# Attention over image rows on one core: P x of two groups between their score matmuls, and its copies in front of the second maximum

## The reference

```python
xn = (x - moving_mean) * jax.lax.rsqrt(moving_var + BN_EPS) * gamma + beta
q = xn @ Wq + bq
k = xn @ Wk + bk
v = xn @ Wv + bv
scores = jnp.einsum('bhid,bhjd->bhij', q, k) * d ** (-0.5)
attn = jax.nn.softmax(scores, axis=-1)
out = jnp.einsum('bhij,bhjd->bhid', attn, v)
out = out @ Wo + bo
return xn + out
```

## Time and profile before

| | us |
|---|---|
| median of 3 runs | 4872.09 (4872.04 to 4872.81) |
| profiled execution | 4878.3 |
| its span, from the first to the last instruction | 4876.3 |

### The profile page before, as it was taken

One profiled execution on the slowest core, in us unless ns is written; L12 is line 12 of the kernel. 1 busy time (PEld: TensorE's weight loads), 2 busy tenths in 40 slices (PEclk: granted clock), 3 DMA queues, 4 the chain that ended last, 5 costly groups with the idle time before them and its releaser, 6 DMA issues.

```text
span 4876.3 us, 170133 instructions
## 1 busy us (share of the span) xinstructions
PE 4840.4 (99%) x51224; PEld 4029.0 (83%) x51224; DVE 4403.0 (90%) x6946; ACT 4332.4 (89%) x18949; POOL 4511.3 (93%) x2824
## 2 busy tenths in 40 slices
PE   7999999999999999999999999999999999999999
PEld 5888888888888888888888888888888888888887
DVE  6999999999999999999999999999999999999998
ACT  6888888888888889888888888888889888888887
POOL 6999999999999999999999999999999999999997
PEclk9999999999999999999999999999999999999999
DMA  7888888888888888888888888888888888888886
GB/s 132 168 168 166 168 165 168 167 166 166 167 167 167 167 167 166 168 168 166 168 166 168 166 166 167 167 167 167 167 167 166 168 168 167 168 166 168 166 166 136
DMA packets 4294233, 806.24 MB, mean 165 GB/s; under 512 B 4294208, under 2 KB 4294208, under 8 KB 4294208
## 3 DMA queue, kind: packets, MB, share of 16 engines
q1 hardware_dynamic: 4293312, 805.80, 83.9%
q10 hardware_dynamic: 896, 0.13, 0.0%
HBM read 537.10 MB, written 268.44 MB: 165 GB/s over the span
## 4 chain that ended last, share of the span: by engine, by line
PE 99%; DVE 0%; ACT 0%; issue 0%; DMA 0%; SPq 0%; DVEq 0%
PE probsT_ps L634 21%; PE score_ps L601 21%; PE uo_ps L618 20%; PE uo_ps L654 19%; PE g_ps L644 18%; ACT probs L329 0%; DMA bias_col<-in_L_conv_bv 0%; ACT g L356 0%; ACT probsT L344 0%; PE uo_ps L582 0%; SPq L191 0%; DVE row_stat L479 0%; DVE probsT L526 0%; DVE y L465 0%; DVE xT L536 0%
## 5 line engine op out<-in xcount | busy, mean ns | idle before, releaser
L329 ACT ACTIVATE probs<-score_ps,neg_top 128x128 f32<-128x128 f32 x8192 | 2916.2, 385 | 479.6 <-DVE neg_top L489 479.6
L271 POOL TENSOR_TENSOR x_weighted<-x_in,row_weights 128x1024 f32<-128x1024 f32 x1024 | 2401.7, 2368 | 21.9 <-DVE x_weighted L432 21.9
L329 ACT ACTIVATION_READ_ACCUMULATOR probs<-score_ps,neg_top 128x1 f32 x8192 | 1836.2, 224 | 0.0
L479 DVE TENSOR_REDUCE row_stat<-score_ps 128x8 f32<-128x1024 f32 x1024 | 1250.4, 1221 | 221.8 <-PE score_ps L601 197.6
L293 POOL TENSOR_TENSOR y<-attn,x_scaled_rows 128x512 f32<-128x512 f32 x768 | 979.8, 1276 | 338.6 <-DVE attn L445 338.6
L634 PE MATMUL probsT_ps<-ident,probs 128*128 128x128 f32 x8192 | 1272.1, 278 | 5.3 <-ACT probsT L344 4.0
L654 PEld LDWEIGHTS uo_ps<-w_o,uT 128*128 128x128 f32 x8192 | 1075.0, 191 | 243.3 <-issue 242.8
L634 PEld LDWEIGHTS probsT_ps<-ident,probs 128*128 128x128 f32 x8192 | 925.1, 141 | 413.2 <-issue 364.5
L282 POOL TENSOR_TENSOR x_scaled_rows<-x_weighted,out_bias 128x512 f32<-128x512 f32 x1024 | 1197.3, 1193 | 0.0
L654 PE MATMUL uo_ps<-w_o,uT 128*128 128x128 f32 x8192 | 1164.4, 275 | 0.0
L644 PE MATMUL g_ps<-xT,w_g 128*128 128x512 f32 x2048 | 1053.9, 596 | 8.2 <-ACT g L356 4.7
(11 more groups left out here) (68 smaller groups left out, 1381.2 us busy)
## 6 DMA issues: line engine op xcount, KB each, us to landing
x_quads<-in_x SPq DMA_DIRECT2D x4096, 64.0 KB, 2.2
x_in<-in_x SPq DMA_DIRECT2D x1024, 256.0 KB, 3.4
out<-y SPq DMA_DIRECT2D x1024, 256.0 KB, 2.4
norm_row<-in_L_conv_gamma ACTq DMA_DIRECT2D x1, 32.0 KB, 2.7
norm_row<-in_L_conv_beta ACTq DMA_DIRECT2D x1, 32.0 KB, 3.6
norm_row<-in_L_conv_bo SPq DMA_DIRECT2D x1, 32.0 KB, 3.1
norm_row<-in_L_conv_moving_mean ACTq DMA_DIRECT2D x1, 32.0 KB, 3.2
norm_row<-in_L_conv_moving_var ACTq DMA_DIRECT2D x1, 32.0 KB, 4.0
```

The source lines that it names most:

```text
L271: nc.gpsimd.tensor_tensor(x_weighted[:, n % 4, :, 0:2 * C].rearrange("p s (h c) -> p s h c", h=2), x_in[:, n % 8, :, None, :].broadcast_to ...
L329: last = nc.scalar.activation(probs[:, n % 4, q, :], score_ps[n % 2][:, q // PAIRS, q % PAIRS * W:(q % PAIRS + 1) * W], ACT.Exp, bias=neg_ ...
L479: nc.vector.tensor_reduce(row_stat[:, s, :, NEG_MAX].rearrange("p (h k) -> p h k", h=2), score_ps[n % 2][:].rearrange("p h (k w) -> p h k ...
```

## The change

In the lists of three engines pieces change places; nothing is added or taken away, and no semaphore's wait is changed. TensorE: both groups' P x stand between the first and the second group's scores. VectorE: the two copies of P x stand in front of the second maximum. ScalarE: the copy of the first half of P transposed comes one exponential later, for both groups.

```diff
@@ ScalarE, step @@
-                exponentials(r, 2 * t, peeled, range(0, 5))
+                exponentials(r, 2 * t, peeled, range(0, 6))
                 keep_probsT(r, 2 * t - 2, peeled, 0)
-                exponentials(r, 2 * t, peeled, range(5, 6))
+                exponentials(r, 2 * t, peeled, range(6, 7))
                 keep_g(r, 2 * t + 4, peeled)
-                exponentials(r, 2 * t, peeled, range(6, 8))
-                exponentials(r, 2 * t + 1, peeled, range(0, 4))
+                exponentials(r, 2 * t, peeled, range(7, 8))
+                exponentials(r, 2 * t + 1, peeled, range(0, 5))
                 keep_probsT(r, 2 * t - 1, peeled, 0)
-                exponentials(r, 2 * t + 1, peeled, range(4, 8))
+                exponentials(r, 2 * t + 1, peeled, range(5, 8))
                 keep_probsT(r, 2 * t - 1, peeled, 1)
                 keep_g(r, 2 * t + 5, peeled)
@@ VectorE, step @@
                 find_shift(r, 2 * t, peeled)
-                find_max(r, 2 * t + 1, peeled)
                 keep_u(r, 2 * t - 4, peeled)
                 keep_u(r, 2 * t - 3, peeled)
+                find_max(r, 2 * t + 1, peeled)
                 find_shift(r, 2 * t + 1, peeled)
@@ TensorE, step @@
                 scores(r, 2 * t, peeled)
-                scores(r, 2 * t + 1, peeled)
                 probs_times_x(r, 2 * t - 4, peeled)
                 probs_times_x(r, 2 * t - 3, peeled)
+                scores(r, 2 * t + 1, peeled)
                 transpose_probs(r, 2 * t - 2, peeled, 0)
```

## The result

| | before, us | after, us |
|---|---|---|
| median | 4872.07 (4872.01 to 4872.81, 4 runs) | 5016.43 (5015.73 to 5017.48, 4 runs) |
| profiled execution | 4878.3 | 5015.96 |
| its span | 4876.3 | 5014.0 |

The changed kernel takes 1.0296 times as long (95% interval 1.0278 to 1.0314). By the medians it lost 144 us, by the profiled spans 137.7: the profiled execution of before was 6 us above its median, that of after at its median. 137.7 us are 0.27 a step; 0.20 was forecast.

What follows compares the result with a forecast made beforehand. TensorE was taken to bound the kernel, busy 99% of the span, with 512 steps of 9.41 us. One more row-shape entry, 0.20 x 512 = 102 us, on 4872.1 gave 4974 us, range 4950 to 5030.

Steps and rivals of the forecast that it cites:

- jitter where three paths meet: Heavier case: three paths meet within 0.02 us before the scores, so every jitter counts; range's upper end 5030.
- TensorE's own work, +0.20: TensorE: one more entry into the scores' row shape costs 0.20 us a step, own work 9.29 to 9.49.
- The bound of 0 for a change from column to row: P x to second scores on TensorE: lowest bound for the new boundary, 0 if the array overlapped the two shapes.
- rival C: TensorE boundaries: first half, new shape change is free; second, the 0.12 wait goes too; 4811 us, chance 0.03.
- The return from row to full size: TensorE after the second scores: left at 0.15 us, the same as from column to full.
- TensorE's wait of 0.12 for ScalarE: Before the scores' last transposes, TensorE waits 0.12 us every step for ScalarE's copy; without it a step is 9.29.
- ScalarE moves by 0.20, not less than 0.18: ScalarE's L344 copies come 0.20 us later, never less than 0.18; its loop goes from 9.41 to 9.61.
- VectorE's copy 0.57 late, a new wait of 0.13: VectorE's copy L526 comes 0.57 us later; TensorE waits 0.13 before the second group's first transposes.
- the transpose of x 0.08 after that: VectorE: transpose of x starts 0.08 us after the second shift, at 2020.07, leading to copy L526 at 2021.23.
- The new wait takes the old one's place: TensorE's 0.13 wait replaces the 0.12 instead of adding: TensorE arrives after 9.62 us, ScalarE after 9.61.
- The sum: Whole kernel: 0.20 us times 512 steps is 102 us, added to the median of 4872.1, gives 4974 us.
- A: Heavier rival: the late VectorE copy is not absorbed, 0.33 us a step, 5041 us; 5000 to 5050 given 0.16.

Runs made afterwards that it cites:

- E6: Changed kernel with VectorE's transpose of x in front of the second maximum and ScalarE's second L344 copy after four exponentials instead of five: 4908.9 us, 1.0054.
- E9: Kernel of before with VectorE finding the first group's maximum and shift in two halves, and ScalarE's first L344 copy after six exponentials: 4811.11 us, 0.9873.
- E2: Changed kernel with VectorE's transpose of x moved in front of the second maximum: 4979.04 us, 1.022.
- E4: Kernel of before with ScalarE's second L344 copy after three instead of four exponentials of the second group: 4881.39 us, 1.002.
- E3: Changed kernel with ScalarE's order of before (first copy after five exponentials, second after four): 5015.11 us, 1.0293.
- E5: Changed kernel with the semaphore waits of VectorE's transpose of x put in front of its second copy of P x: 4984.46 us, 1.021.
- E1: Changed kernel with the semaphore waits of VectorE's transpose of x put in front of the second maximum: 5027.48 us, 1.0318.

## Why the prediction was right, and where it fell short

The range (4950 to 5030) and the direction held, and so did the mechanism, with one term too small. That the range still held is in part luck: its upper end was set for jitter where three paths meet, not for a queue that is late. Point by point:

- **TensorE's own work, +0.20.** Right: the second score visit takes 1.09 like the first, and E6 less E9 gives 0.19. The forecast's 0.20 came from a pitch of 0.112; 0.79 / 7 is 0.113, which would give 0.18: the last hundredths of it are rounding. The bound of 0 for a change from column to row is excluded, and with it the first half of rival C. The return from row to full size costs the same 0.15 as from column to full (0.58 and 0.59). The Trainium skill's exception, in "TensorEngine Tiling (Array Packing)", "Key Properties" (a change of tiling mode drains the engine), agrees with these traces in that a price stands at each boundary, the new one included; that a drain is what it pays for is not shown apart.
- **TensorE's wait of 0.12 for ScalarE.** Right: it went in the changed kernel and came back in E2. What I had not seen is a second place of the same loop with only 0.08 of cover (E4).
- **ScalarE moves by 0.20, not less than 0.18.** E2 stands at 9.61, where this put it. E3 shows that the order of ScalarE's list changes nothing in the changed kernel.
- **VectorE's copy 0.57 late, a new wait of 0.13.** The chain of reasoning was right and one link was mis-sized: "the transpose of x 0.08 after that" took the distance from a place where two copies ran ahead of the shift. It measured 0.11 in two of four steps and 0.21 in the other two, which makes the wait 0.16 and 0.26 (E5: 0.14 at a distance of 0.10).
- **The new wait takes the old one's place.** Right up to 9.61 to 9.64, and that was all the cover there was: the two paths were forecast to meet within 0.01, so each further 0.01 on VectorE went into the time in full. (0.16 + 0.26) / 2 = 0.21; less the 0.12 that went and with 0.20 for the shape it makes 0.29 a step. The spans' 0.27 is a little less since in one of four steps of before the scores took 0.03 to 0.06 longer:

```profile
2033.42 2.05 PE score_ps L601 x32
```

- **The sum.** 4974 against 5016: 42 us short, of which E2 (4979) recovers 37 by taking VectorE's lateness away.
- **The rivals.** The result lies between forecast and A. A named the right place and the right signature, three paths that meet, but took the whole 0.12 to stay on top; it went, and VectorE's wait grew instead.

The Trainium skill, "VectorE: DVE Perf Modes", section "The DRAIN you can't avoid", reports a chain of copies that took the same time with a semaphore after each as with one at the end. These traces don't contradict it where the waits stand behind running work (E5), and limit it: with nothing left running beside it, one more entry of the queue cost 0.10 us where it was a register operation (0.21 against 0.11, after) and 0.09 where it was a wait (0.14 against 0.05, E1).

## What to carry to other kernels

When an instruction is moved, its neighbours' gaps don't move with it: a distance read from a trace holds only with the same work in front, since VectorE's queue here worked off waits and register operations beside the instruction that ran, and in the open when that one was short (0.18). Where several paths are forecast to meet within a few hundredths, the sum is a lower bound, not a middle. And before a list is reordered around a wait, look for the next deadline on the same loop (E4); shortening the loop itself, as by handing on half of a maximum (E9), meets all of them at once.

## What the runs showed of the hardware that was not expected

- A transpose of x with three semaphore waits started 0.08 us after a shift of 0.17 us when these waits had been worked off before, 0.11 after it when one queued wait stood between, and 0.21 in the two of four steps in which a register operation (line 532) stands there too.
- Waits written ahead of an instruction join that instruction's own, and their order is not the written one: in E1 the wait for the second scores is written last and was worked off ahead of one of the three that are written in front of it, which then cost 0.09 us in the open.
- A change from column to row shape costs what one from full size does (1.09 for both score visits), and from row to full what one from column does.
- The kernel of before took 4872 us on one chip and 4882 on another, while E6, in which TensorE waits for nobody, took on the slower of them the 4909 that its step gives (512 x 9.49 = 4859 and the 50 us of filling and emptying that before has too). Why is open.
